# A two-layer decoder in one kernel: the MLP four batches wide and the second cross attention in pairs of batches, both in split float32r, and the exponents' sums taken on ScalarE

## The chip, the cores and the metric

One core of a Trainium2 chip runs the whole program. The metric is the device time of one execution in microseconds (us), as the median of several runs. TensorE (PE, with its weight loads shown as PEld), VectorE (DVE), ScalarE (ACT) and GpSimd (POOL) each run a queue of their own in order; SyncE (SP) starts the DMAs.

## The reference

The input `x` is 16 batches of 128 tokens with 256 features. Six layers follow each other, each with a layer norm in front and added to `x`: causal attention, cross attention with a norm of q and k, gated MLP, grouped attention, cross attention with a mask, and an MLP with quantised operands. The two layers that change most compute this (all in float32):

```python
# gated MLP: shared and routed experts
def _mlp(x, gw, uw, dw):
    g = x @ gw.T
    u = x @ uw.T
    return g * jax.nn.sigmoid(g) * u @ dw.T
logits = x.astype(jnp.float32) @ router_weight.astype(jnp.float32).T
topk_vals, topk_idx = jax.lax.top_k(logits, TOP_K)
topk_w = jax.nn.softmax(topk_vals, axis=-1)
...
shared = _mlp(x, sh_gate, sh_up, sh_down)      # 1024 inner features
routed = _mlp(x, r_gate, r_up, r_down) * comb_w[:, None]   # 128 inner features
# second cross attention: 16 heads of 128, 8 key heads
scores = jnp.einsum('bhtd,bhsd->bhts', q, k) / scale
scores = jnp.where(mask, scores, -jnp.inf)
attn = jax.nn.softmax(scores, axis=-1)
out = jnp.einsum('bhts,bhsd->bhtd', attn, v)
return out @ Wo
```

The first cross attention is the same without a mask, with an RMS norm of each head's q and k and 16 key heads.

## The kernel before

The layers run one after the other, each in a block of its own with code for every engine; between blocks all engines meet. Inside a layer the order of the work is written out by hand: a `step` function per engine names the work of one batch, with parts for the batch before and after, and semaphores (`wait_ge`, `then_inc`) tie the engines together. `x` stays in SBUF. The weights of the next layer are loaded while a layer runs.

**The first cross attention** (`normed_cross_attention`) and **the second** (`masked_cross_attention`) fold weights first (in the second, the q and k weights into `wqk`, v and output into `wo`), and then take each batch in 4 groups of 4 heads, 64 groups in all. For a group `i` of the second: `project_q` (L1419, ordinary float32, 128 columns a product) fills a bank, ScalarE copies it (`copy_qT`, L1272), `scores` adds a mask product (L1426) and four score products (L1429), VectorE takes the row maxima (L1328) and makes the shift, ScalarE four exponents (L1278), VectorE their sums (L1335) and reciprocals, GpSimd divides (L1236), TensorE turns the result (L1403), ScalarE copies it (`copy_probsT`, L1285), TensorE weighs the context (L1443), ScalarE copies the heads (L1290), and TensorE projects them into the batch's output (`add_output`, L1452, 256 columns). The groups overlap: TensorE in step `i` does scores of `i`, q of `i + 1`, turns the weights of `i - 1`, adds the output of `i - 2` and weighs the context of `i - 1`. ScalarE in the same step: heads of `i - 2`, exponents of `i`, q of `i + 1`, turned weights of `i - 1`. In between VectorE and GpSimd quantise a slice of the last layer's weights (`scale_slice`, `round_slice`). The first is built alike, with more work for the norms: scores L1079, maxima L946, exponents L882, sums L966, reciprocals L969, copies L876 (turned weights), L899 (heads), L904 and L909 (k and q), output L1100. Its projections are already split: a float32 operand is the sum of a high and a low float32r part, and a product is three float32r products, high by high, high by low and low by high (`PARTS`, L1046).

**The MLP** (`gated_mlp`) takes one batch after the other. With the batch's `hT` (256 features, 128 tokens) 36 products of 128 columns give gate and up (L1628), 2 of 8 columns the router's logits (L1638); ScalarE takes a tanh (L1544), VectorE two multiplications (L1569, L1574), and 9 products of 256 columns project down (L1616, L1620). Statistics of the new `x` for the next layer's norm follow (L168 to L172), with a power on GpSimd (L133). All is ordinary float32. The last layer's gate and up products (L2262) are split float32r of 512 columns.

## Time and profile before

| what | value |
|---|---|
| three runs of the kernel | 1809.45, 1809.5, 1805.52 us |
| the profiled execution | 1805.99 us |
| its span, first to last instruction | 1803.2 us |
| mean granted TensorE clock | 0.973 of 2.4 GHz |
| TensorE busy | 1664.0 us, 92% |
| VectorE, ScalarE, GpSimd busy | 1108.6, 779.1, 694.4 us |

Times in the trace count from the first instruction. In it TensorE's work is a list of MATMUL records; an ordinary float32 product shows as two records, a float32r or bfloat16 product as one. A record's duration is the time until its result is there; the next record starts earlier, so what a product costs in a row of products is the distance between starts.

### The profile page before, as it was taken

What the parts mean: (1) busy time and instruction counts of PE and PEld (TensorE: products, weight loads), DVE (VectorE), ACT (ScalarE), POOL (GpSimd) and SP (SyncE); (2) the same over time, 40 slices, a digit from 0 to 9 for tenths busy, and PEclk for the clock granted to TensorE, in tenths of its full rate; (3) what the DMA queues carried; (4) which work ended last, traced back from release to release, by engine and by line L of the source; (5) the groups of instructions that cost most, each with busy time, mean ns of one, the idle gap of its engine ahead of it and who ended that gap; (6) DMA issues with size and microseconds to landing.
All of it is one profiled execution on the core that took longest, in us unless ns stands there. A gap on an engine that the chain in (4) does not pass through costs nothing. (4 is left out here: it accounts for less than half of the span.)

```text
span 1803.2 us, 33598 instructions
## 1 busy us (share of the span) xinstructions
PE 1664.0 (92%) x10928; PEld 1316.5 (73%) x10928; DVE 1108.6 (61%) x2520; ACT 779.1 (43%) x1788; POOL 694.4 (39%) x884
## 2 busy tenths in 40 slices
PE   4999879999999998999978888889999999978887
PEld 2555558888888887999945555488888888767676
DVE  3566546676776763455445666545555565489996
ACT  1433446767676763111124444334444444432221
POOL 3566634555545451000022222103233333357775
PEclk8999989999999999999979999999999999989998
DMA  5000020000000000000030000010000000000000
GB/s 213 1 0 0 1 82 4 3 3 3 1 3 1 3 2 20 1 0 0 0 117 1 0 0 0 6 74 7 6 6 6 6 6 5 1 4 12 9 12 12
DMA packets 15633, 28.43 MB, mean 16 GB/s; under 512 B 1745, under 2 KB 12242, under 8 KB 14802
## 3 DMA queue, kind: packets, MB, share of 16 engines
q1 hardware_dynamic: 15570, 27.63, 4.3%
q8 instruction: 35, 0.57, 0.1%
q14 instruction: 28, 0.23, 0.0%
HBM read 25.53 MB, written 2.10 MB: 15 GB/s over the span
## 5 line engine op out<-in xcount | busy, mean ns | idle before, releaser
L1236 POOL TENSOR_TENSOR weights_even<-weights_even,cross_reciprocal 128x512 f32<-128x512 f32 x64 | 66.9, 1045 | 283.4 <-DVE cross_reciprocal L1340 283.4
L133 POOL TENSOR_TENSOR rstd<-variance,minus_half 128x1 f32 (+1 forms) x80 | 44.1, 551 | 335.3 <-DVE variance L172 335.3
L843 POOL TENSOR_TENSOR weights_odd_early<-weights_odd_early,cross_reciprocal 128x512 f32<-128x512 f32 x64 | 66.7, 1042 | 190.2 <-DVE cross_reciprocal L969 190.2
L1628 PE MATMUL bank<-mlp_hT,weights_even 128*128 128x128 f32 x1152 | 138.1, 280 | 0.5 <-ACT mlp_hT L151 0.5
L1628 PEld LDWEIGHTS bank<-mlp_hT,weights_even 128*128 128x128 f32 x1152 | 135.2, 195 | 1.5 <-ACT mlp_hT L151 0.8
L1032 PEld LDWEIGHTS bank<-ident,weights_odd_early 128*128 128x128 f32 x768 | 93.7, 141 | 45.1 <-issue 32.7
L1419 PE MATMUL bank<-cross_hT,cross_wqk 128*128 128x128 f32 x1024 | 124.9, 275 | 0.6 <-ACT cross_hT L1266 0.6
L1100 PE MATMUL bank<-weights_odd_early 128*128 128x256 f32 x512 | 121.4, 380 | 1.6 <-ACT weights_odd_early L899 1.6
L1452 PE MATMUL bank<-weights_even 128*128 128x256 f32 x512 | 121.2, 380 | 0.7 <-ACT weights_even L1290 0.7
L1419 PEld LDWEIGHTS bank<-cross_hT,cross_wqk 128*128 128x128 f32 x1024 | 119.5, 192 | 0.9 <-ACT cross_hT L1266 0.9
L1032 PE MATMUL bank<-ident,weights_odd_early 128*128 128x128 f32 x768 | 115.1, 273 | 2.9 <-DVE weights_odd_early L955 2.9
L1847 DVE TENSOR_REDUCE grouped_maxima<-bank 128x4 bf16<-128x512 f32 x128 | 82.3, 685 | 55.5 <-PE bank L1913 55.5
L1278 ACT ACTIVATE weights_even<-bank,cross_shift 128x128 f32<-128x128 f32 x256 | 73.2, 369 | 74.4 <-DVE cross_shift L1330 73.7
L1761 ACT ACTIVATE grouped_probs<-bank 128x512 f32<-128x512 f32 x128 | 67.6, 599 | 83.1 <-PE bank L1931 83.1
L1100 PEld LDWEIGHTS bank<-weights_odd_early 128*128 128x128 f32 x512 | 92.3, 190 | 13.4 <-ACT weights_odd_early L899 3.5
L1452 PEld LDWEIGHTS bank<-weights_even 128*128 128x128 f32 x512 | 92.3, 190 | 11.4 <-ACT weights_even L1290 1.5
L882 ACT ACTIVATE weights_odd_early<-bank,cross_shift,cross_q_rms 128x128 f32<-128x128 f32 x256 | 96.1, 458 | 1.7 <-DVE cross_shift L949 1.7
L1328 DVE TENSOR_REDUCE cross_maxima<-bank 128x4 f32<-128x512 f32 x64 | 44.2, 691 | 78.5 <-PE bank L1429 78.3
L367 POOL TENSOR_TENSOR causal_masked_maxima<-causal_maxima,causal_constants 128x512 bf16<-128x512 bf16 x64 | 67.7, 1080 | 63.1 <-DVE causal_maxima L492 63.1
L1335 DVE TENSOR_REDUCE cross_sums<-weights_even 128x4 f32<-128x512 f32 x64 | 43.9, 686 | 77.5 <-ACT weights_even L1278 77.5
L1046 PE MATMUL bank<-high_weights,cross_high 128*128 128x512 f32 x192 | 87.0, 453 | 1.2 <-DVE cross_low L978 1.2
L1290 ACT ACTIVATE weights_even<-bank 128x512 f32<-128x512 f32 x64 | 38.3, 598 | 113.1 <-PE bank L1443 113.1
(272 smaller groups left out, 4177.8 us busy)
## 6 DMA issues: line engine op xcount, KB each, us to landing
weights_odd_early<-in_weights SPq DMA_DIRECT2D x2, 3072.0 KB, 13.4
weights_even<-in_weights SPq DMA_DIRECT2D x2, 2560.0 KB, 12.7
weights_even<-in_weights SPq DMA_DIRECT2D x2, 1732.0 KB, 8.9
weights_odd_late<-in_weights SPq DMA_DIRECT2D x2, 1536.0 KB, 8.6
x<-in_x SPq DMA_DIRECT2D x4, 512.0 KB, 6.0
cross_context<-in_context SPq DMA_DIRECT2D x32, 64.0 KB, 1.8
out<-mx_result SPq DMA_DIRECT2D x16, 128.0 KB, 1.7
weights_even<-in_weights SPq DMA_DIRECT2D x2, 512.0 KB, 8.6
```

The lines of the kernel that those rows point to most:

```text
L367: pool.tensor_tensor(masked_maxima[g][:, :, :], maxima[s][:, g, :].unsqueeze(2).to_broadcast([P, PER, P]), later.unsqueeze(1).to_broadcast ...
L882: last = act.activation(probs[x][:, j, :], bank_scores[:, j * P:(j + 1) * P], ACT.Exp, scale=q_rms[x][:, j:j + 1], bias=shift[x][:, j:j + 1])
L1032: last = pe.transpose(bank[:, j * P:(j + 1) * P], source, core.ident[:, :])
L1046: last = pe.matmul(out, half[:, c, :], split_weights[b][:, at:at + PER * D], start=(k == 0), stop=(k == len(jobs) - 1))
L1100: last = pe.matmul(bank_y[:, 0:EMBED], headsT[x][:, j, :], wo[:, h, :], start=(h == 0), stop=(h == HEADS - 1))
L1236: pool.tensor_tensor(probs[x], probs[x], reciprocal[x][:, :].unsqueeze(2).to_broadcast([P, PER, P]), ALU.mult).then_inc(probs_divided, 1)
L1278: last = act.activation(probs[x][:, j, :], bank_scores[x][:, j * P:(j + 1) * P], ACT.Exp, scale=SCALE, bias=shift[x][:, j:j + 1])
L1419: last = pe.matmul(bank_q[:, j * P:(j + 1) * P], wqk[:, c, h * D:(h + 1) * D], hT[s][:, c, :], start=(c == 0), stop=(c == EC - 1))
L1452: last = pe.matmul(bank_y[s][:, 0:EMBED], headsT[x][:, j, :], wo[:, h, :], start=(h == 0), stop=(h == HEADS - 1))
L1628: last = pe.matmul(out, wt[:, c, m * P:(m + 1) * P], layer.hT[:, c, :], start=(c == 0), stop=(c == EC - 1))
L1761: act.activation(probs[:, SLOTS * c + j, :], bank_scoresT[j][:, :], ACT.Exp, scale=SCALE)\
L1847: dve.tensor_reduce(maxima[s][:, g * PER:(g + 1) * PER], bank_scores[j].rearrange("p (h k) -> p h k", h=PER), AX.X, ALU.max).then_inc(max_ ...
```

## The change

In both cross attentions each exponent gets `accum_out`: ScalarE writes the sum of the row beside the exponents, and the reductions on VectorE (L966, L1335) go. The exponents wait also for the reciprocals (in the second, the lifted sums) of the group before last.

The second cross attention takes two batches at once, in 8 groups of 2 heads for each of 8 pairs. `hT` of both, the folded weights and the heads are split into a high part (a copy on ScalarE) and a low part (a remainder on VectorE); q's projection and the output projection are three float32r products of 256 columns. Mask, score, transpose and context products stay as they are. ScalarE's order changes: it copies the turned weights before q.

The MLP takes four batches at once. The routed expert becomes the first of 9 tiles of 128 inner features; for a tile, gate and up are 2 x 6 float32r products of 512 columns (four batches' tokens), and the tile is projected down for each batch with 3 of 256 columns, two tiles later. The weights are split at the layer's start, slice by slice; the inner values get their high part from ScalarE and their low part from GpSimd. The loop is written out instead of looped over.

```diff
             def exponentials(i, x):
                 act.wait_ge(shift_ready, i + 1)
                 act.wait_ge(probsT_filled, nonneg(i - 1))
+                act.wait_ge(reciprocal_ready, nonneg(i - 1))
                 for j in range(PER):
                     last = act.activation(probs[x][:, j, :], bank_scores[:, j * P:(j + 1) * P], ACT.Exp,
-                                          scale=q_rms[x][:, j:j + 1], bias=shift[x][:, j:j + 1])
+                                          scale=q_rms[x][:, j:j + 1], bias=shift[x][:, j:j + 1],
+                                          accum_out=sums[x][:, j:j + 1])
                 last.then_inc(probs_ready, 1)
...
             def reciprocals(i, x):
                 dve.wait_ge(probs_ready, i + 1)
-                dve.tensor_reduce(sums[x][:, :], probs[x], AX.X, ALU.add).then_inc(sums_ready, 1)
-                dve.wait_ge(sums_ready, i + 1)
                 dve.wait_ge(probs_divided, nonneg(i - 1))
                 dve.reciprocal(reciprocal[x][:, :], sums[x][:, :]).then_inc(reciprocal_ready, 1)
...
+    BOTH = 2
+    GROUPS = 8
     PER = HEADS // GROUPS
+    JOBS = PER * BOTH
...
+            for k in range(FUSED):
                 act.wait_ge(fused_filled, k + 1)
-                act.activation(fused_weights(k), core.banks[k % 8][:, :], ACT.Copy).then_inc(fused_ready[0], 1)
-
-            def copy_hT(b, s):
+                act.activation(fused_weights(k, 0), core.banks[k % 8][:, :], ACT.Copy).then_inc(fused_high, 1)
...
+                act.wait_ge(lifted_ready, nonneg(i - 1))
+                for j in range(JOBS):
                     last = act.activation(probs[x][:, j, :], bank_scores[x][:, j * P:(j + 1) * P], ACT.Exp,
-                                          scale=SCALE, bias=shift[x][:, j:j + 1])
+                                          scale=SCALE, bias=shift[x][:, j:j + 1], accum_out=sums[x][:, j:j + 1])
                 last.then_inc(probs_ready, 1)
...
-            def copy_headsT(i, x):
+            def copy_high_heads(i, x):
                 act.wait_ge(out_filled, i + 1)
                 act.wait_ge(added, nonneg(i - 1))
-                act.activation(headsT[x], four(bank_out), ACT.Copy).then_inc(headsT_ready, 1)
+                act.activation(heads[x][0][:, :, :], four(bank_out), ACT.Copy).then_inc(heads_high, 1)
 
             def step(t, s):
                 for g in range(GROUPS):
                     i = GROUPS * t + g
                     if there(i - 2):
-                        copy_headsT(i - 2, g % 2)
-                    if g == 1 and batch_there(t + 1):
-                        copy_hT(t + 1, 1 - s)
+                        copy_high_heads(i - 2, g % 2)
                     if there(i):
                         exponentials(i, g % 2)
+                    if g in (2, 5) and pair_there(t + 1):
+                        k = (g - 2) // 3
+                        copy_hT(BOTH * (t + 1) + k, t + 1, 1 - s, k)
+                    if there(i - 1):
+                        copy_probsT(i - 1, (g - 1) % 2)
                     if there(i + 1):
                         copy_qT(i + 1, (g + 1) % 2)
-                    if there(i - 1):
-                        copy_probsT(i - 1, (g - 1) % 2)
-            batches_in_turn(act, step)
+            pairs_in_turn(act, step)
...
+                dve.wait_ge(fused_high, k + 1)
+                dve.tensor_tensor(fused_weights(k, 1), core.banks[k % 8][:, :], fused_weights(k, 0).bitcast(F32),
+                                  ALU.subtract).then_inc(fused_low, 1)
...
+            def make_low_heads(i, x):
+                dve.wait_ge(heads_high, i + 1)
+                dve.tensor_tensor(heads[x][1][:, :, :], four(bank_out), heads[x][0][:, :, :].bitcast(F32),
+                                  ALU.subtract).then_inc(heads_low, 1)
...
+                jobs = [(c, a, b) for c in range(EC) for a, b in PARTS]
                 for j in range(PER):
                     h = g * PER + j
-                    for c in range(EC):
-                        last = pe.matmul(bank_q[:, j * P:(j + 1) * P], wqk[:, c, h * D:(h + 1) * D], hT[s][:, c, :],
-                                         start=(c == 0), stop=(c == EC - 1))
+                    for m, (c, a, b) in enumerate(jobs):
+                        last = pe.matmul(bank_q[:, j * BOTH * P:(j + 1) * BOTH * P],
+                                         wqk_split[b][:, c, h * D:(h + 1) * D],
+                                         hT[s][a][:, c, :, :].rearrange("p b t -> p (b t)"),
+                                         start=(m == 0), stop=(m == len(jobs) - 1))
                 last.then_inc(q_filled, 1)
...
+                jobs = [(k, j, a, b) for k in range(BOTH) for j in range(PER) for a, b in PARTS]
+                for m, (k, j, a, b) in enumerate(jobs):
+                    last = pe.matmul(bank_y[s][:, k * EMBED:(k + 1) * EMBED], heads[x][a][:, k * PER + j, :],
+                                     wo_split[b][:, g * PER + j, :], start=(g == 0 and m == 0),
+                                     stop=(g == GROUPS - 1 and m == len(jobs) - 1), skip_group_check=True)
                 last.then_inc(added, 1)
...
+            def low_inner(i):
+                pool.wait_ge(inner_high, i + 1)
+                pool.wait_ge(tile_down, downs(i - 2))
+                pool.tensor_tensor(halves[i % 2][1][:, :], inner[i % 2][:, :],
+                                   halves[i % 2][0][:, :].bitcast(F32), ALU.subtract).then_inc(inner_low, 1)
...
+            def high_inner(i):
+                act.wait_ge(inner_ready, i + 1)
+                act.wait_ge(tile_down, downs(i - 2))
+                act.wait_ge(inner_low, nonneg(i - 1))
+                act.activation(halves[i % 2][0][:, :], inner[i % 2][:, :], ACT.Copy).then_inc(inner_high, 1)
...
+            def gate_and_up(i, k):
+                if i < TILES:
+                    pe.wait_ge(weights_low, k + 1)
+                pe.wait_ge(inner_ready, nonneg(i - 1))
+                jobs = [(c, a, b) for c in range(EC) for a, b in PARTS]
+                for which, bank in enumerate((bank_gate[i % 2], bank_up[i % 2])):
+                    for m, (c, a, b) in enumerate(jobs):
+                        at = k * PER_TILE + (which * EC + c) * P
+                        last = pe.matmul(bank[:, :], split_weights[b][:, at:at + P], hT[a][:, c, :],
+                                         start=(m == 0), stop=(m == len(jobs) - 1))
+                last.then_inc(tile_filled, 1)
+
+            def down(q, k):
+                i = TILES * q + k
+                at = k * PER_TILE + 2 * EC * P
+                pe.wait_ge(inner_low, i + 1)
+                if k == 0:
+                    pe.wait_ge(top_ready, q + 1)
+                if k == 1:
+                    pe.wait_ge(layer.x_updated, QUAD * q)
+                for j in range(QUAD):
+                    for m, (a, b) in enumerate(PARTS):
+                        if k == 0:
+                            start, stop = m == 0, m == len(PARTS) - 1
                         else:
-                            pe.wait_ge(inner_ready, nonneg(PARTS * (t - 1) + k + 1))
-                            for m in range(PER):
-                                project(bank_gate[j][:, m * P:(m + 1) * P], w_gate, j * PER + m)
-                            for m in range(PER):
-                                last = project(bank_up[j][:, m * P:(m + 1) * P], w_up, j * PER + m)
-                        last.then_inc(part_filled, 1)
-            pipeline(pe, step)
+                            start, stop = k == 1 and m == 0 and j % 2 == 0, k == LAST and m == len(PARTS) - 1
+                        last = pe.matmul(y_of(bank_h if k == 0 else bank_y, j),
+                                         halves[i % 2][a][:, j * P:(j + 1) * P], split_weights[b][:, at:at + EMBED],
+                                         start=start, stop=stop, skip_group_check=(k > 0))
+                    if k == LAST or j == QUAD - 1:
+                        last.then_inc(tile_down, 1)
+
+            turn_h(0)
+            for q in range(QUADS):
+                route(q)
+                for k in range(TILES):
+                    gate_and_up(TILES * q + k, k)
+                    if q > 0 and k == 0:
+                        down(q - 1, LAST)
+                    if k >= 2 and k < LAST:
+                        down(q, k - 2)
+                if q + 1 < QUADS:
+                    turn_h(q + 1)
+                down(q, LAST - 2)
+                down(q, LAST - 1)
+            down(QUADS - 1, LAST)
```

ScalarE in the second cross attention, in a step that also copies a batch's context and h; first before, then after (L1290 and L1321 copy heads, L1272 and L1302 q, L1285 and L1316 the turned weights, L1278 and L1309 are the exponents):

```order
L1290 ACTIVATE weights_even<-bank 128x512
L1265 ACTIVATE cross_contextT<-bank 128x128
L1266 ACTIVATE cross_hT<-bank 128x256
L1278 ACTIVATE weights_even<-bank,cross_shift 128x128 x4
L1272 ACTIVATE weights_even<-bank 128x512
L1285 ACTIVATE weights_even<-bank 128x512
```

```order
L1321 ACTIVATE cross_high_heads<-bank 128x512
L1309 ACTIVATE weights_even,cross_sums<-bank,cross_shift 128x128 x4
L1295 ACTIVATE cross_contextT<-bank 128x128
L1296 ACTIVATE cross_high_hT<-bank 128x2x128
L1316 ACTIVATE weights_even<-bank 128x512
L1302 ACTIVATE weights_even<-bank 128x512
```

The copies of context and h now stand behind the exponents, the copy of the turned weights stands directly behind them, and q's copy is last; each exponent also writes to `cross_sums`.

VectorE in the first cross attention, one step without statistics, before and after:

```order
L942 TENSOR_REDUCE cross_k_sums<-weights_odd_early 128x4
L946 TENSOR_REDUCE cross_maxima<-bank 128x4
L949 SCALAR_TENSOR_TENSOR cross_shift<-cross_maxima,cross_q_rms 128x4
L955 TENSOR_TENSOR weights_odd_early<-bank,cross_k_rms 128x512
L962 TENSOR_SCALAR weights_odd_early<-bank 128x512
L966 TENSOR_REDUCE cross_sums<-weights_odd_early 128x4
L969 RECIPROCAL cross_reciprocal<-cross_sums 128x4
L974 TENSOR_REDUCE cross_q_sums<-weights_odd_early 128x4
```

```order
L944 TENSOR_REDUCE cross_k_sums<-weights_odd_early 128x4
L948 TENSOR_REDUCE cross_maxima<-bank 128x4
L951 SCALAR_TENSOR_TENSOR cross_shift<-cross_maxima,cross_q_rms 128x4
L957 TENSOR_TENSOR weights_odd_early<-bank,cross_k_rms 128x512
L964 TENSOR_SCALAR weights_odd_early<-bank 128x512
L969 RECIPROCAL cross_reciprocal<-cross_sums 128x4
L974 TENSOR_REDUCE cross_q_sums<-weights_odd_early 128x4
```

The reduction into `cross_sums` is gone and the reciprocal follows the copy of q.

TensorE in the MLP: before, the change from one batch to the next (transposes, down, gate and up, router); after, the end of an up product and the start of the down products of an earlier tile:

```order
L145 MATMUL bank<-ident,mlp_h 128x128 x2
L1616 MATMUL bank<-weights_even,mlp_inner 128x256
L1620 MATMUL bank<-weights_even,mlp_inner 128x256 x8
L1628 MATMUL bank<-mlp_hT,weights_even 128x128 x4
L1638 MATMUL bank<-weights_even,mlp_hT 128x8 x2
L1628 MATMUL bank<-mlp_hT,weights_even 128x128 x32
```

```order
L1815 MATMUL bank<-mlp_high_hT,mlp_high_weights 128x512
L1815 MATMUL bank<-mlp_high_hT,mlp_low_weights 128x512
L1815 MATMUL bank<-mlp_low_hT,mlp_high_weights 128x512
L1833 MATMUL bank<-mlp_high_weights,mlp_high_inner 128x256
L1833 MATMUL bank<-mlp_low_weights,mlp_high_inner 128x256
L1833 MATMUL bank<-mlp_high_weights,mlp_low_inner 128x256
```

Products of 128 columns by one batch have given way to float32r products of 512 columns by four batches, with the weights as the stationary operand, and the down products stand between the tiles.

## Rows read from the trace of the kernel before

**Rows 1.** The page, part 1: busy us, share of the span, instructions.
```profile
PE 1664.0 (92%) x10928; PEld 1316.5 (73%) x10928; DVE 1108.6 (61%) x2520; ACT 779.1 (43%) x1788; POOL 694.4 (39%) x884
```

**Rows 2.** Stages: window, busy us by engine (instructions), granted clock, DMA share, GB/s.
```profile
230.80:700.90 470.10, 458.84 (x2576) 377.82 (x2576) 314.60 (x644) 315.26 (x660) 227.60 (x335) 0.99 0.03 10
701.90:912.00 210.10, 206.11 (x1536) 195.80 (x1536) 101.64 (x304) 31.34 (x80) 8.26 (x15) 0.98 0.01 4
912.90:1168.50 255.60, 219.94 (x1728) 128.70 (x1728) 144.86 (x336) 106.58 (x256) 56.95 (x100) 0.95 0.06 21
1168.50:1580.30 411.80, 402.59 (x2640) 347.98 (x2640) 224.06 (x553) 189.01 (x488) 120.45 (x129) 0.99 0.04 13
1580.40:1803.20 222.80, 186.45 (x848) 151.06 (x848) 192.70 (x361) 57.50 (x109) 149.58 (x145) 0.93 0.03 10
```

**Rows 3.** Timeline, first cross attention: start, duration, engine, line, operands, count [idle before].
```profile
426.10 1.50 ACT L882 ACTIVATE weights_odd_early<-bank,cross_shift,cross_q_rms 128x128 f32<-128x128 f32 x4
...
427.63 0.69 DVE L966 TENSOR_REDUCE cross_sums<-weights_odd_early 128x4 f32<-128x512 f32 x1
...
428.27 0.58 ACT L899 ACTIVATE weights_odd_early<-bank 128x512 f32<-128x512 f32 x1
...
429.24 1.89 PE L1100 MATMUL bank<-weights_odd_early 128*128 128x256 f32 x8
...
430.97 1.05 PE L1079 MATMUL bank<-weights_odd_early 128*128 128x128 f32 x8
...
432.99 1.50 ACT L882 ACTIVATE weights_odd_early<-bank,cross_shift,cross_q_rms 128x128 f32<-128x128 f32 x4
```

**Rows 4.** Timeline, second cross attention, one group and the next one's start.
```profile
1404.80 0.38 PE L1426 MATMUL bank<-cross_mask_diagonal,ones_bf 128*128 128x512 bf16 x1
...
1405.91 1.95 PE L1419 MATMUL bank<-cross_hT,cross_wqk 128*128 128x128 f32 x16
...
1407.04 1.14 ACT L1278 ACTIVATE weights_even<-bank,cross_shift 128x128 f32<-128x128 f32 x4 [1.36 <-DVE cross_shift L1330]
...
1407.70 0.60 PE L1403 MATMUL bank<-ident,weights_even 128*128 128x128 f32 x4
...
1408.06 0.61 ACT L1272 ACTIVATE weights_even<-bank 128x512 f32<-128x512 f32 x1
1408.13 1.89 PE L1452 MATMUL bank<-weights_even 128*128 128x256 f32 x8
...
1408.54 0.62 ACT L1285 ACTIVATE weights_even<-bank 128x512 f32<-128x512 f32 x1
...
1409.86 1.02 PE L1443 MATMUL bank<-weights_even,cross_context 128*128 128x512 f32 x2
...
1410.72 0.38 PE L1426 MATMUL bank<-cross_mask_diagonal,ones_bf 128*128 128x512 bf16 x1
...
1412.53 0.38 ACT L1266 ACTIVATE cross_hT<-bank 128x256 f32<-128x256 f32 x1
```

**Rows 5.** Timeline, quantised MLP: float32r products of 512 columns in a row.
```profile
1589.39 0.39 PE L2262 MATMUL bank<-mx_high_weights,mx_low_hT 128*128 128x512 f32 x1
...
1589.62 0.40 PE L2262 MATMUL bank<-mx_high_weights,mx_high_hT 128*128 128x512 f32 x1
1589.62 0.19 PEld L2262 LDWEIGHTS bank<-mx_low_weights,mx_high_hT 128*128 128x128 f32 x1
```

**Rows 6.** By line, ScalarE: count, duration in ns (least, median, most), first and last start.
```profile
L882 ACT ACTIVATE weights_odd_early<-bank,cross_shift,cross_q_rms x256: 446/457/474, 252.5 to 691.5; 128x128 f32<-128x128 f32 x128
...
L1278 ACT ACTIVATE weights_even<-bank,cross_shift x256: 359/368/382, 1193.4 to 1569.6; 128x128 f32<-128x128 f32 x128
...
L1548 ACT ACTIVATE mlp_router<-mlp_router x16: 203/204/205, 707.6 to 900.6; 128x1 f32<-128x1 f32 x16
```

**Rows 7.** The page, part 5 (GpSimd), and the timeline of the MLP's end (VectorE).
```profile
L1236 POOL TENSOR_TENSOR weights_even<-weights_even,cross_reciprocal 128x512 f32<-128x512 f32 x64 | 66.9, 1045 | 283.4 <-DVE cross_reciprocal L1340 283.4
...
905.73 0.69 DVE L1569 SCALAR_TENSOR_TENSOR mlp_gated<-mlp_tanh,bank 128x512 f32<-128x512 f32 x1 [2.08 <-ACT mlp_tanh L1544]
```

578 lines of the change are left out of this document (344 added, 234 removed).

## The prediction

> **What bounds the kernel now.** Read the busy shares of the page first: TensorE is busy for 92% of the span, nothing else for more than 61% [rows 1]. The table by stages shows where [rows 2]: its rows are the first cross attention, the MLP, the grouped attention, the second cross attention and the quantised MLP. In the three that the change touches TensorE is busy for 459 of 470.1 us, 206 of 210.1 and 403 of 411.8. So they last as long as their matmuls, and no other engine is near its limit as a share: ScalarE has 315 us in the first cross attention and 189 in the second. The share hides something, though: both attentions run a ring through ScalarE in each of their 64 groups (scores, maxima, exponents, copies, the matmul that needs the copy), and the change lengthens that ring. So the second thing to read is the slack of the ring, in the timelines.
>
> First cross attention [rows 3]: the exponents of one group begin at 426.10 and of the next at 432.99, a period of 6.89 (one group in four takes 7.22, for the next batch's transposes). The first exponent starts 2.02 after the scores (430.97 to 432.99). After the exponents ScalarE squares, then copies the heads; that copy ends at 428.27 + 0.58 = 428.85, and the output projection that needs it starts at 429.24. A woken TensorE starts about 0.05 later than what it waits for, so 0.34 us of slack. Then come 1.73 us of projection and the next scores: nothing more is in the ring.
>
> Second cross attention [rows 4]: the period is 5.92 (1404.80 to 1410.72), 6.25 with transposes, 6.00 on average; TensorE has no gap.
>
> **Prices of matmuls.** From the starts in [rows 4]: sixteen records of 128 columns, ordinary float32, take 1.79 us, 0.112 each, and a product is two records: 0.224. Four products of 256 columns take 1.73, 0.432 each; transposes 0.43 for four, 0.109 each; the two of 512 columns 0.86. A float32r product of 512 columns takes 0.230 [rows 5], one record. The change needs 256 columns of float32r, which the trace does not have. A float32r record of 512 columns costs 0.014 more than an ordinary record of 256 (0.216); half of the one should cost about the same more than half of the other, so I take 0.12, between 0.112 (the 128-column record, which brings a weight load too) and, far off, the 0.19 that a weight load lasts [rows 5] if it were not hidden.
>
> **MLP.** Now each batch has 36 products of 128 columns and 9 of 256. Afterwards four batches go together: 9 tiles x 2 x 6 = 108 float32r products of 512 columns, 108 x 0.230 = 24.8; down 9 x 4 x 3 = 108 of 256 columns, 13.0; 8 transposes 0.9; 24 small routing products at the 0.11 of a record, 2.6. That is 41.3, four times 165.2. Around it: four normalisations before the first transpose, then two copies and two remainders before the first product, some 3.7 us more than the transposes counted; the third tile's weight remainder stands behind the gate and the top-two on VectorE, 1.5; the last tile's chain (tanh 0.6, two gate steps of 0.69, copy 0.6, GpSimd's remainder at the 1.05 of its 512-column instructions [rows 7], hand-overs) outlasts the 24 down products in front of it by 1.3; additions and statistics of four batches behind the last product 5.1, with the power 0.5 longer. The granted clock of 0.98 in this stage [rows 2] is some 7 us at 1.2 instead of 2.4 GHz, after the idle change of layers; it costs about 3 us in both. Together 180, against 210.1: **-29 us**. Ends: -31 at 0.112 a product, 0 at 0.19. Splitting the weights (nine slices, 0.8 us of ScalarE and 1.0 of VectorE each) lies under the first four batches' 4.2 us a tile, and so do the remainders on GpSimd, 1.05 a tile. If that cover were gone, each tile would wait for the rest of its 3.6 us chain; a tile's down product comes two tiles later, so it isn't.
>
> **Second cross attention, TensorE's side.** A group is two heads of two batches instead of four heads of one. The mask product and four score products stay (0.22 + 0.90), so do transposes 0.44 and the two context products 0.86. Projection of q: 8 x 0.224 = 1.79 becomes 12 x 0.12 = 1.44; output: 4 x 0.432 = 1.73 becomes 1.44. Sum 5.37 with the transposes of h, against 6.00: 64 x 0.63 = -40. Fusing now copies all 16 banks on ScalarE and makes 16 remainders of 0.72 on VectorE beside 14 us of TensorE (32 products at 0.224, 16 at 0.432); the last remainder and the first pair's two batches come late, +3 to +4. So -36, if TensorE stays the bound. VectorE gives up a sum of 0.69 a group and takes on a remainder of 0.69.
>
> **Sums with the exponents.** This is what decides. The order shows the sums as a second output of each exponent, four times a group in both attentions, 512 in all. No row has such an instruction. The Trainium skill (VectorE: DVE Perf Modes, section "Two Vector instructions with no wait between them") says for VectorE that an op which also writes its accumulator is two instructions, the op and an accumulator read; no run here shows it. My price, a, is the time that each exponent's turn grows by. The nearest row is the shortest ScalarE instruction, the one-column exponential of 0.203 us [rows 6]. A plain one would hide about 0.11 of that: four exponents of 0.368 take 1.14 rather than 1.47 [rows 4, 6]. Hidden at both of its sides, a = 0.09, the same as what a second operand in a column costs (0.457 - 0.368 [rows 6]). If it waits for the exponent's end and only its own end is hidden, a = 0.20; if neither, 0.31. Below nothing isn't possible, since nothing is taken off ScalarE. I take 0.20: the read needs the finished sum, while the next exponent doesn't need the read.
>
> First cross attention: the sum of VectorE that goes (0.69, L966 [rows 3]) wasn't in the ring, since the projection doesn't wait for it. So the layer gains nothing, and pays 4a - 0.34 a group: 0.46 x 62 = **+28 us** at 0.20; +1 at 0.09; +56 at 0.31. The added wait on reciprocal_ready stands in front of the exponents with group i-1's count, long reached; the square of q, three copies and the square of k are queued behind it and lose nothing.
>
> Second: in the new order ScalarE runs exponents(i), then copies the turned weights of i-1, then q of i+1. Scores to exponents 2.24 (1404.80 to 1407.04), exponents 1.14 + 4a, the copy 0.60 of which 0.12 is overlapped, hand-overs 0.2, the context products 0.86, then the next scores: 4.9 + 4a. At 0.20 that is 5.7, above the 5.29 of a group without transposes. Two groups in eight put the copies of context and h between (the longer one 0.38 [rows 4]; some 0.5 together), one comes late for quantising: 5.85 on average. 64 x (5.85 - 6.00) = -10, and with the slower start and end **-4 us**. At 0.09: 5.5 on average, -28. At 0.31: 6.3, +25.
>
> **The sum.** 28 - 29 - 4 = -5 on the profiled execution's own 1806 (span 1803.2 and 2.8 around it): 1801. The three runs shown lie at 1805.5, 1809.45 and 1809.5; the profiled one is at their lower end, and I leave the forecast at 1801.
>
> **Rivals.** *The reads are hidden like any short instruction* (a up to 0.15): -56 at 0.09, with TensorE the bound in all three layers, so 1750; -30 at 0.15. For it: every ScalarE instruction in the rows overlaps its neighbour. Against: those don't need the neighbour's result. *The reads are hidden nowhere*, on the other side: from a = 0.22 the kernel is slower than now, at 0.31 by +56 - 29 + 25 = +52, so 1858. The place is ScalarE between the first exponent and the copy behind it, in both rings. For it: nothing but the dependence on both sides; against: the next exponent reads another bank slice. *256-column products are bound by their weight load*, 0.19: 24 a group x 0.07 puts the second attention at 7.05 a group, +67, the MLP's gain goes, with the first attention +95: 1900. Against: an ordinary 128-column record has the same load and a pitch of 0.112. The skill (TensorE: Matmul & The Clock Gate, section "LDWEIGHTS (loading the stationary operand)") puts a load of 128 columns at 107 ns, which would just fit under such a product; the trace's 0.112 agrees. *The change doesn't do what it says*: TensorE's products move as written, so only the sum's price can undo it.
>
> **How the numbers follow.** Forecast, a from 0.17 to 0.22, -18 to +5: chance 0.40, of that 0.24 faster by over 0.3%, 0.16 within. Hidden reads: 0.30, faster. Unhidden: 0.22, of that 0.02 within. Weight load or something else slow: 0.08, slower but for 0.01. (0.3%, 5.4 us, is what a measurement here can tell from no change.) Faster 0.54, same 0.19, slower 0.27. The range reaches down to 1748, all of the first rival, and up to 1840, most of the second; the forecast's own range is 1788 to 1812.
>
> **What would show it.** Starts of exponents in the first attention: 6.89 apart if I overrate the read, 7.35 by the forecast, and a gap of TensorE before the output projection, ended by ScalarE's copy of the heads. In the second, a gap before the context products, ended by the copy of the turned weights; none if a is 0.09. MLP stage 180 us, float32r products of 256 columns 0.12 apart. I am wrong in mechanism if the exponents grow by less than 0.15 a piece, or if a product of 256 columns takes over 0.14.

## The result, and the profile after

| | before | after |
|---|---|---|
| median | 1808.9 us | 1759.32 us |
| runs | 1805.52 to 1809.5 | 1758.88 to 1762.37 |
| span of the profiled execution | 1803.2 us | 1757.4 us |

The ratio is 0.9739, with a 95% interval of 0.9722 to 0.9756. The changed kernel is 47 us faster by this ratio, and by the two profiled executions (1805.99 and 1759.19 us); the medians of the table lie 49.6 apart. The forecast was 5 us, no change that can be measured. The stated range (1748 to 1840) holds the time only because it reached down to the forecast's first rival (1750, chance 0.30), 9 us below the time; the forecast's own range was 1788 to 1812.

Part 1 of the page of the changed kernel: busy time, share of the span and instructions of each engine, to be held against [rows 1].

```profile
PE 1602.4 (91%) x10512; PEld 1276.1 (73%) x10512; DVE 1055.4 (60%) x2390; ACT 840.0 (48%) x2322; POOL 740.1 (42%) x908
```

TensorE is about as full as before (91% against 92%). ScalarE has 61 us more and 534 instructions more, VectorE 53 us less.

The stages of the changed kernel, with the columns of [rows 2]: window, its length, busy time and instructions of PE, PEld, DVE, ACT and POOL, granted clock, DMA share, GB/s. The rows are the first cross attention, the MLP, the grouped attention, the second cross attention and the quantised MLP.

```profile
228.80:701.70 472.90, 460.75 (x2576) 379.31 (x2576) 274.64 (x580) 325.87 (x916) 229.59 (x336) 0.99 0.03 10
701.70:885.80 184.10, 174.34 (x992) 153.13 (x992) 96.53 (x214) 55.75 (x94) 52.43 (x41) 0.95 0.02 6
885.80:1145.00 259.20, 222.23 (x1728) 130.08 (x1729) 144.87 (x336) 106.94 (x256) 57.29 (x100) 0.93 0.05 21
1145.00:1533.20 388.20, 368.19 (x2768) 346.15 (x2768) 215.64 (x577) 214.29 (x752) 120.92 (x128) 0.99 0.04 15
1533.20:1757.30 224.10, 187.44 (x848) 152.28 (x848) 193.22 (x361) 57.80 (x109) 149.54 (x144) 0.93 0.03 10
```

Measured in both traces from the first instruction of a layer to that of the next (the first cross attention from TensorE's first, some 2 us after GpSimd's): MLP 211.0 to 184.1 (-26.9), second cross attention 411.6 to 388.2 (-23.4), first cross attention 471.2 to 472.9 (+1.7), and in the layers that the change leaves alone -1.9, +3.0 and +1.7. That is the 45.8 us between the spans.

ScalarE in the first cross attention after the change, one group: start, duration, engine, line, operation, operands, count. It answers to [rows 3].

```profile
425.31 0.45 ACT L883 ACTIVATE weights_odd_early<-bank,cross_shift,cross_q_rms 128x128 f32<-128x128 f32 x1
425.65 0.20 ACT L883 ACTIVATION_READ_ACCUMULATOR weights_odd_early<-bank,cross_shift,cross_q_rms 128x1 f32 x1
425.75 0.46 ACT L883 ACTIVATE weights_odd_early<-bank,cross_shift,cross_q_rms 128x128 f32<-128x128 f32 x1
426.09 0.20 ACT L883 ACTIVATION_READ_ACCUMULATOR weights_odd_early<-bank,cross_shift,cross_q_rms 128x1 f32 x1
426.18 0.46 ACT L883 ACTIVATE weights_odd_early<-bank,cross_shift,cross_q_rms 128x128 f32<-128x128 f32 x1
...
426.96 0.21 ACT L883 ACTIVATION_READ_ACCUMULATOR weights_odd_early<-bank,cross_shift,cross_q_rms 128x1 f32 x1
427.05 0.64 ACT L891 ACTIVATE weights_odd_early<-weights_odd_early 128x512 f32<-128x512 f32 x1
427.58 0.61 ACT L901 ACTIVATE weights_odd_early<-bank 128x512 f32<-128x512 f32 x1
...
432.19 0.45 ACT L883 ACTIVATE weights_odd_early<-bank,cross_shift,cross_q_rms 128x128 f32<-128x128 f32 x1
```

The sum is an instruction of its own behind each exponent, ACTIVATION_READ_ACCUMULATOR, 0.20 us long. But it starts 0.34 us after the exponent does (425.31 to 425.65), before the exponent's end at 425.76, just where the next exponent stood before, and the next exponent starts 0.09 or 0.10 behind it. From exponent to exponent it is 0.43 (425.75 to 426.18) where it was 0.343 (four exponents in 1.50 in [rows 3], the last of them 0.47 long). So the price is a = 0.09, and behind 511 of the 512 reads the next instruction starts 0.091 to 0.097 later. The group's period is the old one: 425.31 to 432.19 is 6.88, against 6.89.

The second cross attention, one group and the next one's start, from the timeline of all engines; it answers to [rows 4].

```profile
1362.28 0.38 PE L1475 MATMUL bank<-cross_mask_diagonal,ones_bf 128*128 128x512 bf16 x1
...
1363.62 0.28 PE L1466 MATMUL bank<-cross_low_hT,cross_high_wqk 128*128 128x256 f32 x1
...
1364.52 0.37 ACT L1309 ACTIVATE weights_even<-bank,cross_shift 128x128 f32<-128x128 f32 x1 [1.44 <-DVE cross_shift L1374]
...
1364.69 0.28 PE L1466 MATMUL bank<-cross_low_hT,cross_high_wqk 128*128 128x256 f32 x1
...
1364.79 0.19 ACT L1309 ACTIVATION_READ_ACCUMULATOR weights_even<-bank,cross_shift 128x1 f32 x1
...
1365.91 0.61 ACT L1316 ACTIVATE weights_even<-bank 128x512 f32<-128x512 f32 x1
...
1366.39 0.62 ACT L1302 ACTIVATE weights_even<-bank 128x512 f32<-128x512 f32 x1
...
1366.68 1.03 PE L1496 MATMUL bank<-weights_even,cross_context 128*128 128x256 f32 x4
...
1367.55 0.38 PE L1475 MATMUL bank<-cross_mask_diagonal,ones_bf 128*128 128x512 bf16 x1
```

The period is 5.27 us (1362.28 to 1367.55), and TensorE has no gap in it. Nine float32r products of 256 columns lie between 1363.62 and 1364.69, 0.119 apart. The copy of the turned weights (L1316) ends at 1366.52, 0.16 before the context products that need it (L1496). These did not quite stay as they were: one product of 512 columns (two records in [rows 4]) has become two of 256 (four records), at the same cost of 0.86 to 0.87 us.

### The profile page after: what moved, and what is told of

It reads as the page before. It is cut to its first block and busy times, and to the rows that moved or that the text cites. A ratio compares the mean times of both kernels' runs of the same rounds, so it can differ in the third digit from the quotient of the medians.

```text
span 1757.4 us, 32678 instructions
## 1 busy us (share of the span) xinstructions
PE 1602.4 (91%) x10512; PEld 1276.1 (73%) x10512; DVE 1055.4 (60%) x2390; ACT 840.0 (48%) x2322; POOL 740.1 (42%) x908
## 5 line engine op out<-in xcount | busy, mean ns | idle before, releaser
L1309 ACT ACTIVATE weights_even<-bank,cross_shift 128x128 f32<-128x128 f32 x256 | 90.7, 367 | 102.1 <-DVE cross_shift L1374 102.1
L1100 PE MATMUL bank<-weights_odd_early 128*128 128x256 f32 x512 | 121.7, 380 | 2.1 <-ACT weights_odd_early L901 2.1
L883 ACT ACTIVATE weights_odd_early<-bank,cross_shift,cross_q_rms 128x128 f32<-128x128 f32 x256 | 113.5, 455 | 1.7 <-DVE cross_shift L951 1.7
L1100 PEld LDWEIGHTS bank<-weights_odd_early 128*128 128x128 f32 x512 | 92.2, 190 | 13.9 <-ACT weights_odd_early L901 4.0
L1603 POOL TENSOR_TENSOR mlp_low_inner<-mlp_inner,mlp_high_inner 128x512 fp32r<-128x512 f32 x36 | 48.5, 1347 | 126.3 <-ACT mlp_high_inner L1644 126.3
L876 ACT ACTIVATE weights_odd_early<-bank 128x512 f32<-128x512 f32 x64 | 38.4, 600 | 98.3 <-PE bank L1032 98.3
L1507 PE MATMUL bank<-cross_high_wo,cross_high_heads 128*128 128x256 f32 x256 | 77.9, 304 | 8.1 <-DVE cross_low_heads L1366 7.7
L944 DVE TENSOR_REDUCE cross_k_sums<-weights_odd_early 128x4 f32<-128x512 f32 x64 | 43.9, 686 | 65.3 <-ACT weights_odd_early L896 64.2
L1466 PE MATMUL bank<-cross_high_hT,cross_high_wqk 128*128 128x256 f32 x256 | 78.0, 305 | 1.1 <-DVE cross_low_hT L1361 1.1
L2351 ACT ACTIVATE mx_silu<-bank 128x512 f32<-128x512 f32 x32 | 19.2, 599 | 122.3 <-PE bank L2467 122.3
L1046 PE MATMUL bank<-low_weights,cross_high 128*128 128x512 f32 x192 | 76.3, 397 | 0.0
L1046 PE MATMUL bank<-high_weights,cross_low 128*128 128x512 f32 x192 | 76.1, 396 | 0.0
```

What stands on the lines that cost most here:

```text
L883: last = act.activation(probs[x][:, j, :], bank_scores[:, j * P:(j + 1) * P], ACT.Exp, scale=q_rms[x][:, j:j + 1], bias=shift[x][:, j:j + ...
L1046: last = pe.matmul(out, half[:, c, :], split_weights[b][:, at:at + PER * D], start=(k == 0), stop=(k == len(jobs) - 1))
L1100: last = pe.matmul(bank_y[:, 0:EMBED], headsT[x][:, j, :], wo[:, h, :], start=(h == 0), stop=(h == HEADS - 1))
L1309: last = act.activation(probs[x][:, j, :], bank_scores[x][:, j * P:(j + 1) * P], ACT.Exp, scale=SCALE, bias=shift[x][:, j:j + 1], accum_ou ...
L1466: last = pe.matmul(bank_q[:, j * BOTH * P:(j + 1) * BOTH * P], wqk_split[b][:, c, h * D:(h + 1) * D], hT[s][a][:, c, :, :].rearrange("p b ...
L1507: last = pe.matmul(bank_y[s][:, k * EMBED:(k + 1) * EMBED], heads[x][a][:, k * PER + j, :], wo_split[b][:, g * PER + j, :], start=(g == 0 ...
```

## The experiments

There are ten experiments. The table gives the length of each stage in each trace, from a layer's first instruction to the next layer's (the first cross attention again from TensorE's first), and the ratio to the kernel before with its interval. Three stages that no edit touches show what one trace is worth: the causal attention takes 226.4 to 230.8 us, the quantised MLP 222.1 to 224.2, the grouped attention 256.2 to 261.7.

| kernel | 1st cross | MLP | grouped | 2nd cross | ratio (95%) |
|---|---|---|---|---|---|
| before | 471.2 | 211.0 | 256.2 | 411.6 | 1 |
| after | 472.9 | 184.1 | 259.2 | 388.2 | 0.9739 (0.9722 to 0.9756) |
| after again (e8) | 473.4 | 183.0 | 257.5 | 389.3 | 0.9743 (0.9729 to 0.9757) |
| e1, sums on VectorE | 472.5 | 185.8 | 257.2 | 395.2 | 0.9752 (0.9730 to 0.9774) |
| e2, before with the sums alone | 472.6 | 210.7 | 258.4 | 413.8 | 1.0012 (0.9997 to 1.0026) |
| e3, before with the wide MLP alone | 472.3 | 184.4 | 258.7 | 411.6 | 0.9850 (0.9828 to 0.9873) |
| e4, first attention padded | 490.4 | 183.8 | 259.1 | 388.1 | 0.9819 (0.9798 to 0.9839) |
| e5, second attention padded | 472.7 | 183.9 | 261.7 | 412.2 | 0.9868 (0.9853 to 0.9883) |
| e6, normalisation early | 472.9 | 184.0 | 261.7 | 386.1 | 0.9749 (0.9736 to 0.9762) |
| e7, q's copy first | 472.9 | 184.1 | 261.7 | 418.7 | 0.9916 (0.9901 to 0.9932) |
| e9, both padded | 491.0 | 182.9 | 257.3 | 412.2 | 0.9953 (0.9936 to 0.9969) |
| e10, a wide read | 473.1 | 184.1 | 261.1 | 393.2 | 0.9754 (0.9738 to 0.9770) |

### Which part of the change brings what

**e1: the sums back on VectorE, the rest of the change kept.** In both attentions the edit is this one (here the second's; the wait that the change put in front of the exponents goes too):

```diff
                     last = act.activation(probs[x][:, j, :], bank_scores[x][:, j * P:(j + 1) * P], ACT.Exp,
-                                          scale=SCALE, bias=shift[x][:, j:j + 1], accum_out=sums[x][:, j:j + 1])
+                                          scale=SCALE, bias=shift[x][:, j:j + 1])
...
+                dve.tensor_reduce(sums[x][:, :], probs[x], AX.X, ALU.add).then_inc(sums_ready, 1)
+                dve.wait_ge(sums_ready, i + 1)
```

> The changed kernel, but in both cross attentions VectorE sums the exponents again and ScalarE writes no sum; wide MLP and paired second attention stay. Theory H (the accumulator read is hidden at both sides, 0.09 us an exponent, and the rings had room for it): the first attention goes back by 1 to 2 us to about 471; in the second each group's VectorE work grows by 0.69 us, which matters only in the two groups of a pair where a slice of weights is scaled and the row maxima come late already (0.3 to 1.1 us in six groups): 0.7 us more in 8 to 16 groups, +6 to +10; total 1764 to 1768. Theory G (the sums taken on ScalarE are what makes the kernel faster): most of the 46 us is lost, over 1780. Theory N (the sums matter nowhere): second attention within 1 us of 388, total 1758.

The second attention takes 395.2 us, 7.0 more than in the changed kernel's trace and 5.9 more than in its second trace (e8), as theory H had it. The time of the whole kernel doesn't show this clear of noise: 0.9752 beside 0.9739 and 0.9743, with intervals that overlap. The 7 us rest on the traces. The first doesn't move (472.5). The 1 to 2 us that H gave it back aren't there, so most of the +1.7 of the changed kernel's trace is not the sums' doing. The waits of TensorE between 1170 and 1530 us (who waited, for whom, us in total, times, longest), in e1:

```profile
PE bank L1508 <- DVE cross_low_heads L1365: 12.1, 18, 1.6
```

and in the changed kernel, from 1175 to 1520:

```profile
PE bank L1507 <- DVE cross_low_heads L1366: 4.7, 6, 1.1
```

With a further 0.69 us on VectorE in each group, the remainder of the heads, which the output projection waits for, comes late 18 times instead of 6 (7 times, 6.3 us, in e8). From the first to the last group that is 5.5 us more, and the layer's start is 1.1 longer. So the sums' gain lies on the side of VectorE's order, and e2 shows that it comes only together with the pairs.

**e2: the kernel before with nothing but the sums moved.** The second attention's part:

```diff
+                act.wait_ge(lifted_ready, nonneg(i - 1))
...
                     last = act.activation(probs[x][:, j, :], bank_scores[x][:, j * P:(j + 1) * P], ACT.Exp,
-                                          scale=SCALE, bias=shift[x][:, j:j + 1])
+                                          scale=SCALE, bias=shift[x][:, j:j + 1], accum_out=sums[x][:, j:j + 1])
...
-                dve.tensor_reduce(sums[x][:, :], probs[x], AX.X, ALU.add).then_inc(sums_ready, 1)
-                dve.wait_ge(sums_ready, i + 1)
```

> The kernel before, with nothing changed but the sums: ScalarE writes them with the exponents in both cross attentions, and VectorE's two reductions go. Theory H: first attention 471.1 to 473 as in the changed kernel; second attention 411.6 within 1 us, since the copy of the turned weights ended 0.70 us before the context products that need it and comes 0.36 later; total within 0.3% of the kernel before, +1 to +3. The forecast's price (0.20 an exponent, ring slack 0.34): first attention +28, total +28 or more. Theory G: faster by over 0.3%.

The ratio is 1.0012, and its interval takes in 1. Alone the sums bring nothing. The forecast's price would have shown as 28 us in the first attention, and it is not there. The second attention is 413.8, 2.2 over the kernel before and more than the 1 us that was expected; 1.9 of it lie ahead of the first group, and from the first to the last group the two traces agree (375.6 and 375.4), so it isn't the reads' doing. Why the start is longer stays open.

**e3: the kernel before with the wide MLP alone** (the function `gated_mlp` and the packing of its weights from the changed kernel, both cross attentions from the one before).

> The kernel before, with the wide MLP alone; both cross attentions as before. Step of the forecast: MLP 180 us or -29; the changed kernel's trace has 184, -27. Grouped attention: if the MLP's new end or the memory traffic behind it is what made it 3 us longer in the changed kernel (granted clock 0.93 instead of 0.95), it is 259 here too and the total is -24; if that was this one execution's clock, it is 256 to 259 without pattern and the total is -27 within 3.

184.4 us in the MLP and 27 us in all (0.9850). On the grouped attention it is 258.7, and over all traces it lies between 256.2 and 261.7 with the same code. Its length goes with the time for which the granted clock was 0.5, that is 1.2 GHz, in it: 27.5 to 28.7 us where the layer takes 256.2 to 257.5, 31.5 to 33.9 where it takes 258.4 to 259.2, and 39.3 to 39.9 where it takes 261.1 to 261.7. Besides, TensorE waits for one transfer (`grouped_rows`) for 5.6 us in the two traces with the old MLP and for 6.7 to 6.9 in the ten with the wide one, so about 1 us may be the wide MLP's. The pairs' share follows from e1: second attention 411.6 to 395.2, -16.4 with VectorE's sums, and 7 more with ScalarE's.

### Was the price of the read all that was wrong?

The read cannot be made slower, but a stand-in can be put beside it: one more ScalarE instruction of one column ahead of each exponent.

```diff
                 for j in range(PER):
+                    for m in range(1):
+                        act.activation(pad[x][:, 4 * m + j:4 * m + j + 1], core.ident[:, 0:1], ACT.Copy)
                     last = act.activation(probs[x][:, j, :], bank_scores[:, j * P:(j + 1) * P], ACT.Exp,
```

**e4: this in the first cross attention.**

> The changed kernel, with one more ScalarE instruction of one column (a copy into a spare column that nobody reads) ahead of each of the 256 exponents of the first cross attention: a stand-in for an accumulator read that costs twice as much, 0.18 us an exponent. Nothing is left out. The forecast's formula (the ring of the first attention has 0.34 us of room over the kernel before, growth 4a - 0.34): +0.38 a group over before, 62 groups, so first attention 494. Room read from the changed kernel's trace (the heads' copy ends 0.25 before the output projection, 0.05 for the wake, so 0.20 left): +0.16 a group, +10, first attention 483. If the added instruction is not 0.09 but 0.2 a piece: +0.6 a group, 510. If the ring isn't the bound at all: 473.

ScalarE and, from 449.26 on, TensorE, in e4's timeline:

```profile
447.05 0.19 ACT L886 ACTIVATE cross_pad<-ident 128x1 f32<-128x1 f32 x1
...
447.14 0.45 ACT L887 ACTIVATE weights_odd_early<-bank,cross_shift,cross_q_rms 128x128 f32<-128x128 f32 x1
447.48 0.20 ACT L887 ACTIVATION_READ_ACCUMULATOR weights_odd_early<-bank,cross_shift,cross_q_rms 128x1 f32 x1
...
447.57 0.20 ACT L886 ACTIVATE cross_pad<-ident 128x1 f32<-128x1 f32 x1
447.67 0.45 ACT L887 ACTIVATE weights_odd_early<-bank,cross_shift,cross_q_rms 128x128 f32<-128x128 f32 x1
...
448.62 0.59 ACT L905 ACTIVATE weights_odd_early<-bank 128x512 f32<-128x512 f32 x1
...
449.26 0.73 PEld L1104 LDWEIGHTS bank<-weights_odd_early 128*128 128x128 f32 x4 [0.23 <-ACT weights_odd_early L905]
```

The copy into the spare column has the read's length and the read's turn: 0.09 (447.05 to 447.14). Exponents are now 0.53 apart (447.14 to 447.67), a = 0.18. TensorE waits for the heads' copy in each group: that copy ends at 449.21 and the weight load that reads it starts 0.05 later. One group earlier, four transposes at 0.109 from 441.55 on are over at 441.99, and the projection starts at 442.13, 0.14 later. The products behind the wait take longer. In e4 and then in the changed kernel, TensorE's rows of the output projection (L1104, L1100), of its weight loads, and of the scores behind it:

```profile
441.55 0.60 PE L1036 MATMUL bank<-ident,weights_odd_early 128*128 128x128 f32 x4
442.12 1.59 PEld L1104 LDWEIGHTS bank<-weights_odd_early 128*128 128x128 f32 x8 [0.21 <-ACT weights_odd_early L905]
442.13 1.99 PE L1104 MATMUL bank<-weights_odd_early 128*128 128x256 f32 x8
443.96 1.05 PE L1083 MATMUL bank<-weights_odd_early 128*128 128x128 f32 x8
...
451.10 1.05 PE L1083 MATMUL bank<-weights_odd_early 128*128 128x128 f32 x8
```

```profile
428.33 1.60 PEld L1100 LDWEIGHTS bank<-weights_odd_early 128*128 128x128 f32 x8
428.44 1.89 PE L1100 MATMUL bank<-weights_odd_early 128*128 128x256 f32 x8
430.17 1.05 PE L1079 MATMUL bank<-weights_odd_early 128*128 128x128 f32 x8
```

From the start of the projection to the scores it is 1.83 us (442.13 to 443.96) and not 1.73 (428.44 to 430.17): TensorE that had to wait needs 0.10 more for the same eight records. The loads show where it goes. In the changed kernel the first weight load starts 0.11 ahead of its product (428.33), beside the last transpose; in e4 it has to wait for the heads, which are these weights, and starts with its product (442.12). The second product then follows 0.32 behind the first instead of 0.22, and all others are 0.216 apart in both. The period is 7.14 (443.96 to 451.10), 0.25 more than before, and the stage 490.4: between the two expectations, 494 and 483.

**e5: the same in the second cross attention.**

> The changed kernel, with one more ScalarE instruction of one column (0.09 us in a row of instructions, as measured in the first attention) ahead of each of the 256 exponents of the second cross attention. Nothing is left out. The ring of exponents, turned weights and context products grows by 0.37 a group. Room in the changed kernel's trace: the copy of the turned weights ends 0.16 before the context products, and 0.06 in the groups that also copy context and h; 0.05 of it is wake. TensorE that had to wait needs 0.10 more to restart, as in the first attention. So 48 x (0.37 - 0.11 + 0.10) + 16 x (0.37 + 0.10) = +25, second attention 413, less what the groups lose that already wait for the low heads: 408 to 413. The forecast's formula (4.9 + 4a against 5.27, without restart): +22, 410. If TensorE stays the bound in spite of it: 389.

412.2 us, +24, inside the expectation. The room of 0.11 and the 0.10 more behind a wait cancel: the growth of 0.37 a group shows in full (64 x 0.37 = 24).

**e9: both.**

> The changed kernel with one more one-column ScalarE instruction ahead of each exponent in both cross attentions: the change as it would be if the accumulator read cost 0.18 us an exponent, close to the 0.20 of the forecast. Nothing is left out. If the forecast failed only in the read's price, this kernel lands where the forecast put the changed one: ratio 0.9743 + 0.0078 (padded first attention) + 0.0125 (padded second) = 0.9946, 1797, and first attention 490, second 412; the forecast's own formula at 0.18 gives -34 + 23 + 57 x ((28 + 56) / 0.22 x 0.09 / 57 ...) no closer than 1792 to 1801. If other steps failed too, by errors that cancel, the total is off from 1801 by more than 10.

Measured: 1798.24 us, 0.9953, stages 491.0 and 412.2, against the 1797, 490 and 412 that the text takes from e4 and e5. With a read of 0.18 us the change is one of half a per cent, and 39 of the 42 us between the changed kernel and the forecast are there. That it ends 3 us from the forecast's 1801 is in part luck, for 1801 stands for a read of 0.20. By the forecast's own terms 0.18 gives +23.6 in the first attention, -29 in the MLP and -8.4 in the second (between its -28 and -4), 1792 in all; measured are +19.8, -28.1 and +0.6. So the price is by far the largest error, and the terms beside it were off by up to 9 us in a layer.

### How short is the read, and why

**e10: a read behind an instruction four times as wide.**

```diff
-                act.activation(probsT[x], four(bank_probsT), ACT.Copy).then_inc(probsT_ready, 1)
+                act.activation(probsT[x], four(bank_probsT), ACT.Copy, accum_out=spare[x][:, :]).then_inc(probsT_ready, 1)
```

> The changed kernel; in the second cross attention ScalarE's copy of the turned weights (512 columns) also writes its sum to a spare column that nobody reads. Nothing is left out. The distance from that copy's start to the start of q's copy behind it is 0.48 us now. If the accumulator read costs a fixed short turn whatever the width, it is 0.57; if the read waits for the end of its instruction (0.61) or grows with the width, 0.68 or more. The copy's signal comes with the read, 0.07 later than the copy's own end, inside the room of 0.06 to 0.11: second attention within 3 us of 388 to 389.

ScalarE in e10, the copy of the turned weights (L1318) with its read, and q's copy (L1304):

```profile
1303.96 0.61 ACT L1318 ACTIVATE weights_even<-bank 128x512 f32<-128x512 f32 x1
1304.44 0.22 ACT L1318 ACTIVATION_READ_ACCUMULATOR weights_even<-bank 128x1 f32 x1
1304.53 0.62 ACT L1304 ACTIVATE weights_even<-bank 128x512 f32<-128x512 f32 x1
```

The read starts 0.48 behind the copy, where q's copy stood, and q's copy starts 0.09 later, at 0.57. The turn of a read is 0.09 behind 512 columns as behind 128. It does not wait for the end of its instruction (1303.96 + 0.61 = 1304.57). The stage, though, takes 393.2, 4 to 5 us more, beyond the 3 that were allowed for; in the ratio (0.9754 beside 0.9739) this is not clear of noise. The copy's signal comes with its read, at 1304.66 instead of 1304.57, and the weight load that waits for it starts at 1304.71. Most groups take 5.35 instead of 5.27. The trace shows how, though TensorE has no gap there. The context products in e10 and, above, in the changed kernel (1366.68):

```profile
1304.74 1.11 PE L1498 MATMUL bank<-weights_even,cross_context 128*128 128x256 f32 x4
```

The four records take 1.11 instead of 1.03. Of the context products in e10 nearly all last 1.09 to 1.13, where most of those in the changed kernel last 1.03 or 1.04. As in e4 the first weight load has lost its lead: it starts 0.025 ahead of its product and not 0.11. So what looked like room in the timeline, 0.06 to 0.11 before the products, was in part the lead of that load.

### The order of the second attention

**e7: q's copy ahead of the turned weights again.**

```diff
+                    if there(i + 1):
+                        copy_qT(i + 1, (g + 1) % 2)
                     if there(i - 1):
                         copy_probsT(i - 1, (g - 1) % 2)
-                    if there(i + 1):
-                        copy_qT(i + 1, (g + 1) % 2)
```

> The changed kernel, but ScalarE in the second cross attention copies q of the next group ahead of the turned weights, as the kernel before did. Theory: that copy (0.47 us in a row) now stands in the ring, whose room is 0.11 at most; +0.36 and 0.10 for the restart in each of 64 groups, +25 to +30, second attention 413 to 418, slower than that of the kernel before (411.6). Rival: q's copy was late for the next scores in the changed order and gains as much as the turned weights lose: 388 to 395.

418.7 us, +30, slower than the stage of the kernel before, and just over the 413 to 418 that were expected. TensorE's waits in it, 1175 to 1520:

```profile
PE bank L1496 <- ACT weights_even L1316: 14.3, 49, 0.7
```

So the exchange of two copies on ScalarE carries the whole gain of the pairs, with the reads in the same ring (the old order without the reads was not run): the copy of 0.47 us that stood in the ring does not fit beside products that have become shorter.

**e6: VectorE's normalisation into a gap.** The six waits of the changed kernel for the low heads follow on groups in which VectorE scales a slice of weights. Its rows there, with the remainder of the heads (L1366) at the end:

```profile
1366.06 0.17 DVE L1379 TENSOR_SCALAR cross_lifted<-cross_sums 128x4 f32<-128x4 f32 x1 [0.98 <-ACT weights_even L1309]
...
1366.55 1.16 DVE L138 TENSOR_SCALAR cross_h<-x,mean,rstd 128x256 f32 x1
1367.63 0.54 DVE L694 TENSOR_REDUCE cross_weights_largest<-weights_odd_late 128x12 f32 x1
...
1369.94 0.68 DVE L1372 TENSOR_REDUCE cross_maxima<-bank 128x4 f32<-128x512 f32 x1
...
1370.73 0.69 DVE L1366 TENSOR_TENSOR cross_low_heads<-bank,cross_high_heads 128x512 fp32r<-128x512 f32 x1
```

The normalisation (L138) takes 1.16 us. GpSimd's division starts 0.03 ahead of it and runs beside it:

```profile
1366.52 1.04 POOL L1264 TENSOR_TENSOR weights_even<-weights_even,cross_reciprocal 128x512 f32<-128x512 f32 x1 [4.65 <-DVE cross_reciprocal L1382]
```

Just ahead, VectorE waits 0.98 us for the exponents. The edit puts the normalisation there:

```diff
                     if there(i - 2):
                         make_low_heads(i - 2, g % 2)
+                    if g in (0, 3) and pair_there(t + 1):
+                        layer.dve_normalise(dve, BOTH * (t + 1) + g // 3)
                     if there(i):
                         reciprocals(i, g % 2)
...
-                    if g in (0, 3) and pair_there(t + 1):
-                        layer.dve_normalise(dve, BOTH * (t + 1) + g // 3)
```

> The changed kernel, with VectorE's normalisation of the next pair's batches (two of eight groups) moved ahead of the reciprocals, into 0.98 us that VectorE spends waiting for the exponents, instead of behind them, where it takes 1.16 us beside GpSimd's division and not 0.38, and pushes the scaling of a weight slice into the next group's row maxima. Theory: the six waits of TensorE for the low heads (4.7 us) go, second attention 383 to 385, total -3 to -5. Rival: VectorE's normalisation waits in the new place too and puts the reciprocals and the division off; the division has 2.5 us of room, so no change, 388.

The normalisation and what waits for the heads, in e6:

```profile
1365.50 0.40 DVE L138 TENSOR_SCALAR cross_h<-x,mean,rstd 128x256 f32 x1
```

```profile
PE bank L1507 <- DVE cross_low_heads L1366: 1.7, 3, 1.1
```

0.40 us instead of 1.16, and the waits fall to 1.7 us. The stage is 386.1, 2 to 3 us shorter than in the two traces of the changed kernel; the expectation was 383 to 385, and in the ratio nothing of it can be seen (0.9749 beside 0.9743 on the same chip). It is not shown to be a better kernel.

**e8: the changed kernel again.**

> The changed kernel itself once more, on the chip and beside the runs of the kernel before that the others of this group share, as the measure for the three other kernels. Same as the first time: 1757 to 1763, ratio 0.972 to 0.976. Grouped attention 257 to 259, as in five of the six traces so far, so that the 256.2 of the kernel before is the outlier and not a gain that the change took away.

1756.85 us, ratio 0.9743, grouped attention 257.5: as expected. But the expectation's "outlier" was too simple, since four further traces have 261.1 to 261.7, and the granted clock goes with it (under e3).

## Why the prediction was wrong

Its forecast was -5 us, the change was -47. At a = 0.09 its own terms give -56; the 10 us between that and -46, the difference of the two spans, are 4.6 in the second attention, 2.1 in the MLP, 0.7 in the first attention and 2.8 in layers that the change leaves alone. Step by step:

**The bound** was read rightly: in all three layers the time is still that of TensorE's matmuls.

**Prices of matmuls**: 0.12 for 256 float32r columns, measured 0.119. The rival of the weight load (0.19 a product) is out.

**MLP**: 180 us forecast, 184.1 measured, and 182.9 to 185.8 in the other traces with the wide MLP. A tile takes 4.23 us (4.2 forecast). Missing was part of the slow clock at the start. A window at the start of that stage in the changed kernel, and one in the kernel before (the granted clock is the third number from the end):

```profile
706.50:716.30 9.80, 9.74 (x36) 8.79 (x37) 0.87 (x2) 0.00 (x0) 0.00 (x0) 0.52 0.01 2
```

```profile
701.90:710.30 8.40, 7.22 (x34) 7.01 (x35) 1.18 (x5) 0.86 (x3) 0.00 (x0) 0.59 0.31 103
```

The granted clock is 1.2 GHz from 703.5 to 710.3 before, 6.8 us, and from 702.3 to 715.9 afterwards, 13.7 us, of which TensorE stands still for 2.3; in both traces it falls after TensorE has stood still between the layers. At half the clock that costs, as an estimate, some 3.4 and 5.7 us; the prediction took 3 in both. TensorE stood still for 4.0 us before the first transposes and 1.4 before the first product, behind four normalisations and two remainders; before it was 3.1 and 0.5, behind one normalisation. The rest of the 4.1 us, 1 to 2, stays open.

**Second cross attention**: the formula 4.9 + 4a gives 5.26 at 0.09, the trace has 5.27. For that price the prediction had -28, measured was -23.4. From the first mask product to the last it is 345.4 us, 5.48 a group on average, what the prediction's 5.5 says; before it was 375.4, so the groups bring -30 where 64 x 0.5 = 32 were counted. The start is 3.4 and the end 3.2 us longer, 6.6 where about 4 were counted. The waits of TensorE for the low heads behind a slice of weights, 4.7 us in all, were in the text only as "one comes late for quantising". "VectorE gives up a sum of 0.69 a group and takes on a remainder of 0.69" was right as a sum and hid that the remainder, unlike the sum, is waited for. The text's own -4 at 0.20 has a slip: -10 and the +4 of the start and end are -6.

**First cross attention**: +28 forecast at 0.20. At 0.09 the formula says +1, and the traces show no more: 471.2 to 472.5 in the three without the read, 472.6 to 473.4 in the seven with it and no pad. But the formula 4a - 0.34 was wrong in two terms. Three rows from the timeline of the kernel before, between those of [rows 3], show them: VectorE's copy of q, ScalarE's square of it, and the weight loads of the output projection:

```profile
427.01 0.69 DVE L962 TENSOR_SCALAR weights_odd_early<-bank 128x512 f32<-128x512 f32 x1 [0.21 <-PE bank L1046]
...
427.74 0.63 ACT L889 ACTIVATE weights_odd_early<-weights_odd_early 128x512 f32<-128x512 f32 x1
...
429.13 1.60 PEld L1100 LDWEIGHTS bank<-weights_odd_early 128*128 128x128 f32 x8
```

The square waited for VectorE until 427.70 and started 1.64 after the exponents, where four turns of 0.343 are 1.37, so there was 0.27 of room that the formula leaves out. The other term is too large: the 0.34 was read from the copy's end to the first product, but what needs the heads is the weight load, 0.11 earlier (429.13). From the copy's end at 428.85 that is 0.28, and 0.23 without the 0.05 of the wake. So the growth is 4a - 0.27 - 0.23: nothing at 0.09, and 0.22 at 0.18, where e4 has 0.25 and the formula 0.38.

**Sums with the exponents: the step that failed.** "I take 0.20: the read needs the finished sum, while the next exponent doesn't need the read." The trace has 0.09, which the prediction's own sign ("I am wrong in mechanism if the exponents grow by less than 0.15 a piece") calls a wrong mechanism. Whatever the read needs of the sum, it does not wait for the recorded end of its instruction: it starts 0.34 after a 128-column exponent and 0.48 after a 512-column copy, when that instruction is still running, exactly where the next instruction stood without it. What the engine does inside is not shown. The row that was nearest in kind, the turn of short instructions in a row, gave 0.09, and it stood in the prediction as the bound; a dependence that was only argued moved the forecast away from it, by 51 us. e9 puts the price back to 0.18, and the whole kernel is at 1798.

The Trainium skill (VectorE: DVE Perf Modes, section "Two Vector instructions with no wait between them") says for VectorE that an accumulator output makes two instructions. The trace shows the same on ScalarE, 512 times; the page gives no price, and this case's is 0.09.

**Chances.** 0.40 stood on -18 to +5, and 0.30 on the case that came. The two were told apart by one number that no row showed; the likelier should have been the one that had rows.
